# A macaron block on one core: another order at the start, halves in two banks at the end

## The reference

```
x = x + 0.5 * ffn(layernorm(x))
x = x + attention(layernorm(x))
x = x + 0.5 * ffn(layernorm(x))
ffn:       W1' = W1 + scale * m1(x), W2' = W2 + scale * m2(x)
           m1, m2: outer products of pairs of the sequence's tokens 1 to 16
           gelu(x W1'^T + b1) W2'^T + b2            (512 hidden units)
attention: 16 heads of 64; q and k divided by their rms, times q_rms_w, k_rms_w
           gate = softplus(k . u / |u| / 8)
           scores = q k^T / 8 - distance * softplus(omega) * slope * gate, causal
           softmax(scores) v, then Wproj
```

## Time and profile before

| | us |
|---|---|
| three runs | 773.44, 774.59, 774.47; median 774.47 |
| the profiled execution | 774.06 |
| its span, first to last instruction | 772.3 |
| TensorE busy | 737.8 (96%) |
| VectorE, ScalarE, GpSimd busy | 660.0, 645.6, 643.0 |
| mean granted clock of TensorE | 0.993 |

### The profile page before, as it was taken

One profiled execution on the slowest core, in us unless ns is written; L12 is line 12 of the kernel. 1 busy time (PEld: TensorE's weight loads), 2 busy tenths in 40 slices (PEclk: granted clock), 3 DMA queues, 4 the chain that ended last, 5 costly groups with the idle time before them and its releaser, 6 DMA issues.

```text
span 772.3 us, 25092 instructions
## 1 busy us (share of the span) xinstructions
PE 737.8 (96%) x9301; PEld 527.0 (68%) x9301; DVE 660.0 (85%) x2101; ACT 645.6 (84%) x1424; POOL 643.0 (83%) x751
## 2 busy tenths in 40 slices
PE   3969999999999999999999999999999999999988
PEld 1435777677667777577667777577766876677764
DVE  7699968987989779888989879897889889899955
ACT  5887889888998889987998889988898879986662
POOL 4265889889998989989999899989899899997780
PEclk9999999999999999999999999999999999999998
DMA  7113711533243423454053432434143432434430
GB/s 186 25 34 79 146 23 44 112 85 85 43 111 71 90 53 70 85 111 99 3 124 71 86 84 46 109 78 107 29 94 91 97 84 35 111 70 97 84 44 28
DMA packets 99602, 60.33 MB, mean 78 GB/s; under 512 B 74606, under 2 KB 86384, under 8 KB 99480
## 3 DMA queue, kind: packets, MB, share of 16 engines
q1 hardware_dynamic: 99320, 58.19, 35.1%
q10 hardware_dynamic: 160, 0.52, 0.2%
HBM read 4.74 MB, written 2.10 MB: 9 GB/s over the span
## 4 chain that ended last, share of the span: by engine, by line
PE 71%; ACT 12%; DVE 6%; POOL 5%; issue 4%; DMA 1%; SPq 0%; POOLq 0%; DVEq 0%; ACTq 0%
PE ps L1056 13%; PE ps L1058 12%; PE ps L1057 12%; PE ps L1176 8%; PE ps L1200 7%; PE ps L1201 7%; PE ps L1158 4%; ACT qk L991 3%; PE ps L1202 3%; ACT pt L1016 2%; POOL pt_l L825 1%; ACT hid L933 1%; DVE maxima L1516 1%; PE ps L1073 1%; ACT L933 1%
## 5 line engine op out<-in xcount | busy, mean ns | idle before, releaser
L825 POOL TENSOR_TENSOR pt_l<-pt 128x512 f16<-128x512 f32 x368 | 322.6, 906 | 35.5 <-ACT pt L1016 34.1
L1512 DVE CUSTOM_DVE_ANT_0 masked<-ps,causal_row 128x512 f16<-128x512 f32 x448 | 192.2, 486 | 26.3 <-PE ps L1176 25.4
L1016 ACT ACTIVATE pt<-ps 128x512 f32<-128x512 f32 (+1 forms) x384 | 174.4, 534 | 15.1 <-PE ps L1202 14.5
L851 POOL TENSOR_TENSOR qkn<-qkn,rs 128x512 f32<-128x512 f32 x128 | 130.8, 1049 | 29.6 <-ACT rs L955 29.0
L1200 PE MATMUL ps<-qk 128*128 128x512 f16 (+3 forms) x512 | 146.6, 299 | 0.0
L1201 PE MATMUL ps<-qk 128*128 128x512 f16 (+3 forms) x512 | 146.5, 299 | 0.0
L1056 PE MATMUL ps<-v_buf,pt 128*128 128x65 f16 x1280 | 129.8, 194 | 2.0 <-POOL pt_l L825 1.2
L1057 PE MATMUL ps<-v_buf,pt 128*128 128x65 f16 x1280 | 129.8, 193 | 0.0
L1058 PE MATMUL ps<-v_buf,pt_l 128*128 128x65 f16 x1280 | 129.6, 193 | 0.0
L1056 PEld LDWEIGHTS ps<-v_buf,pt 128*128 128x128 bf16 x1280 | 118.0, 98 | 7.4 <-issue 4.5
L1057 PEld LDWEIGHTS ps<-v_buf,pt 128*128 128x128 bf16 x1280 | 117.5, 98 | 1.7
(11 more groups left out here) (204 smaller groups left out, 1970.6 us busy)
## 6 DMA issues: line engine op xcount, KB each, us to landing
qk<-qk SPq DMA_DIRECT2D x128, 128.0 KB, 2.4
qk<-qk SPq DMA_DIRECT2D x62, 256.0 KB, 3.7
x_in<-in_L_attn_x SPq DMA_DIRECT2D x8, 256.0 KB, 3.1
out<-x_out SPq DMA_DIRECT2D x8, 256.0 KB, 2.5
qk<-qk SPq DMA_DIRECT2D x1, 1024.0 KB, 7.5
qk<-gtt SPq DMA_DIRECT2D x64, 8.0 KB
qk<-nmt SPq DMA_DIRECT2D x64, 2.0 KB
y_hl<-ytt SPq DMA_TRANSPOSE x63, 3.2
```

What stands on the lines that cost most here:

```text
L825: g.tensor_tensor(pt_l[:, h % 2, c], pt[:, h % 2, c], pt_h[:, h % 2, c], ALU.subtract).then_inc(s_pt_l, 1)
L851: g.tensor_tensor(qk, qk, r.unsqueeze(4).broadcast_to([P, 2, 2, 2, D]), ALU.mult).then_inc(s_qkn, 1)
L1016: a.activation(pt[:, h % 2, c], ps[:, j, 0:width], ACT.Exp).then_inc(s_exp, 1)
L1512: ins = d.tensor_tensor_reduce(masked[:, part.unit(s, i)[0], col:col + (ib + 1) * P], part.bank(s, i)[:, col:col + (ib + 1) * P], causal_r ...
```

## The change

It has these parts.

- **ScalarE's lead**: `gp` (the gelu table) goes from the front to behind `m`, directly before the first gelu; `setup` and `zt` go ahead of the qkv weights, `wo` behind `ln1` of the attention.
- **VectorE's lead**: `us` goes ahead of `ln2`, `uu` ahead of `setup`, `wq` 0 and 1 to either side of the first residual sum; the four square sums of the first quad (`qk` 0) all stand ahead of the gate weights.
- **Bias rows**: from VectorE to GpSimd, behind `m`, as four operations with a semaphore between them.
- **Gate weights by halves**: `gu2` 0 and 1, each with its product, reduction, cast and subtraction; `gu2` 1 stands behind the logits of the first half. `s_prepared` counts to 2, and the waits on it follow.
- **TensorE's lead**: `setup` before `m`; the six fillers go from the front to just ahead of the first hidden layer; the eighteen that stood behind the first ffn's output go among the projections (8 behind `qk` 1 1, 10 behind `v` 0 1); the spread of u (`uu`) goes directly behind that output.
- **The first sequence**: the same stages on each engine in a somewhat different order (`first`); for example `pv` 6 and `pv` 10 on TensorE now stand behind `s` 8 and `s` 12, which they preceded. `body` is the same.
- **Token halves in two banks**: the output of the first ffn and of the last, and the last output product of the attention, write token blocks 0 and 1 into their ring bank and 2 and 3 into a second one. `sum_halves` adds each half by itself and takes the next norm's statistics of three of the four blocks in between. The last store is two DMAs.
- **The last y parts in free operand memory**: the transposed y of pairs 6 and 7 goes to `y_end`, in `qk2`, so the last transfer and the last split don't wait for the product before.
- **The last head's low parts** (`pl` 15) are all three VectorE's; `yt` 6 on GpSimd comes directly behind `pl` 14.
- **TensorE's end**: `wp` 2 stands behind the last weighted sum and `yx`; eight fillers stand between `m` and `h` of the last ffn, and the thirteen at the very end are gone. On VectorE the sum of the sequence before (`add`, `c`, LAST) goes from ahead of `weff` into `m`, between the low part of z and the second half of `weff`.

```diff
 "tensor" lead:
-            ("warm", 0, 6, NEXT), ("zt", "a", NEXT), ("m", "a", NEXT), ("setup", NEXT), ("h", "a", NEXT),
-            ("out", "a", NEXT), ("warm", 1, 8, NEXT), ("warm", 1, 10, NEXT), ("zt", "att", NEXT), ("qk", 0, 0, NEXT),
+            ("zt", "a", NEXT), ("setup", NEXT), ("m", "a", NEXT), ("warm", 0, 6, NEXT), ("h", "a", NEXT),
+            ("out", "a", NEXT), ("uu", NEXT), ("zt", "att", NEXT), ("qk", 0, 0, NEXT), ("qk", 0, 1, NEXT),
...
 "tensor" final:
-            ("wp", 2, THIS), ("pv", 15, THIS), ("yx", THIS), ("wp", 3, THIS), ("out", "c", LAST), ("zt", "c", THIS),
-            ("m", "c", THIS), ("h", "c", THIS), ("out", "c", THIS), ("warm", 3, 7, THIS), ("warm", 2, 6, THIS),
+            ("pv", 15, THIS), ("yx", THIS), ("wp", 2, THIS), ("wp", 3, THIS), ("out", "c", LAST), ("zt", "c", THIS),
+            ("m", "c", THIS), ("warm", 2, 8, THIS), ("h", "c", THIS), ("out", "c", THIS),
...
 "scalar" lead:
-            ("gp", "a", NEXT), ("ln1", "a", NEXT), ("sel", NEXT), ("wq", 0, NEXT), ("zt", "a", NEXT), ("setup", NEXT),
+            ("ln1", "a", NEXT), ("sel", NEXT), ("setup", NEXT), ("zt", "a", NEXT), ("wq", 0, NEXT), ("m", "a", NEXT),
+            ("gp", "a", NEXT), ("h", "a", NEXT), ("wq", 1, NEXT), ("wq", 2, NEXT), ("ln1", "att", NEXT), ("wo", NEXT),
...
 "vector" lead:
-            ("ln1", "a", NEXT), ("ln2", "a", NEXT), ("us", NEXT), ("zl", NEXT), ("b2", NEXT), ("setup", NEXT),
+            ("ln1", "a", NEXT), ("us", NEXT), ("ln2", "a", NEXT), ("zl", NEXT), ("uu", NEXT), ("setup", NEXT),
...
+        SECOND_HALF = {"a": Y_BANK, "att": 0, "c": 1}
...
+        y_end = [qk2[:, 0, K1, :, :], qk2[:, 0, Q0, :, :]]
+        y_last = y_end[1]
...
+            def bias_rows(part, s, b):
+                pool.wait_ge(s_wffn, 16 * 7)
+                pool.wait_ge(s_w_l["a"], 1)
...
+                g.tensor_scalar(b2rows[top, :, :], b2ld[top, :].unsqueeze(1).broadcast_to([1, TB, C]), W_UP, None, ALU.mult).then_inc(s_b2_top, 1)
+                g.tensor_scalar(b2cut[low, :], b2ld[low, :], W_UP, None, ALU.mult).then_inc(s_b2_cut, 1)
...
+                g.tensor_scalar(b2ld[low, :], b2ld[low, :], W_UP, None, ALU.mult).then_inc(s_b2_up, 1)
...
+                g.tensor_tensor(b2rows[low, :, :], b2ld[low, :].unsqueeze(1).broadcast_to([1, TB, C]),
+                                b2cut[low, :].unsqueeze(1).broadcast_to([1, TB, C]), ALU.subtract).then_inc(s_b2, 1)
...
+                dve.wait_ge(s_wqk[hf], 64)
+                half_of, heads = slice(hf * 512, (hf + 1) * 512), slice(hf * HH, (hf + 1) * HH)
+                link(d.tensor_tensor(pairs(uk[:, half_of]), wqk_ld[:, 2 * hf:2 * hf + 2, 1, :].rearrange("p q (i n) -> p q i n", i=2),
+                                     pairs(ps[:, hf, :]), ALU.mult))
+                link(d.tensor_reduce(wu[:, heads], of_heads(uk[:, half_of]), AX.X, ALU.add))
+                link(d.tensor_copy(wu_h[:, heads], wu[:, heads]))
+                d.tensor_tensor(wu_l[:, heads], wu[:, heads], wu_h[:, heads], ALU.subtract).then_inc(s_prepared, 1)
...
+            def sum_halves(part, s, n, by, src, dst, next_stats):
+                for t in (0, TB // 2):
+                    if t == 0:
+                        part.full(dve, s)
+                    else:
+                        dve.wait_ge(s_second_half[n], 1)
+                    bank = part.bank(s) if t == 0 else ps[:, SECOND_HALF[n], :]
+                    blocks, cols = slice(t, t + TB // 2), slice(t * C, (t + TB // 2) * C)
+                    ins = d.scalar_tensor_tensor(dst[:, blocks, :].rearrange("p t c -> p (t c)"), bank[:, cols], by,
+                                                 src[:, blocks, :].rearrange("p t c -> p (t c)"), ALU.mult, ALU.add)
...
+                    if next_stats:
+                        for u in range(t, min(t + TB // 2, TB - 1)):
+                            d.bn_stats(stats[next_stats][:, u, :], dst[:, u, :])
...
+                        sp.dma_start(rows[:, 0:TB // 2, :], x_out[:, 0:TB // 2, :]).then_inc(s_out, 16)
+                        sp.wait_ge(s_second_half[n], 2)
+                        sp.dma_start(rows[:, TB // 2:TB, :], x_out[:, TB // 2:TB, :]).then_inc(s_out, 16)
```

More of the change, by code:

```diff
@@ L1101, in ffn_out @@
                 if b == 0 and n == "a":
+                    pe.wait_ge(s_b2_top, 1)
                     pe.wait_ge(s_b2, 1)
                 part.room(pe, s)
-                pe.matmul(part.bank(s), ones[:, :], b2rows[:, :, :].rearrange("p t c -> p (t c)"), start=True, stop=False)
+                for first, dst in ((0, part.bank(s)), (T // 2, ps[:, SECOND_HALF[n], :])) if shared(n, b) else ((0, part.bank(s)),):
+                    width = T // 2 if shared(n, b) else T
+                    pe.matmul(dst[:, first:first + width], ones[:, :], b2rows[:, :, :].rearrange("p t c -> p (t c)")[:, first:first + width],
+                              start=True, stop=False)
                 for r in range(FB):
@@ L1112, in ffn_out @@
                         c = slice(t * P, (t + 1) * P)
-                        mm = product(part.bank(s)[:, c], hid_h[:, r, c], hid_l[:, r, c], w2_h[:, w], w_l[:, 1, w], False,
-                                     r == FB - 1 and t == TB - 1)
-                part.filled_by(mm, s)
+                        second = shared(n, b) and t >= TB // 2
+                        dst = ps[:, SECOND_HALF[n], :] if second else part.bank(s)
+                        mm = product(dst[:, c], hid_h[:, r, c], hid_l[:, r, c], w2_h[:, w], w_l[:, 1, w], False,
+                                     r == FB - 1 and t == (TB // 2 - 1 if shared(n, b) and not second else TB - 1))
+                        if shared(n, b) and r == FB - 1 and t == TB // 2 - 1:
+                            part.filled_by(mm, s)
+                if shared(n, b):
+                    mm.then_inc(s_second_half[n], 1)
+                else:
+                    part.filled_by(mm, s)
             def project_qk(part, s, b, qd, t):
@@ L1188, in scores @@
                 n = b * H + h
+                if n == 0:
+                    pe.wait_ge(s_prepared, 2)
                 if h % QH == 0:
@@ L1459, in add_ffn @@
                     dve.wait_ge(s_out, 16 * b)
+                if shared(n, b):
+                    sum_halves(part, out, n, 0.5 / W_UP, src, dst, "att" if n == "a" else None)
+                    return
                 part.full(dve, out)
```

289 lines of the change are left out of this document (155 added, 134 removed).

## The result

The changed kernel takes 765.4 us (median of 4 runs, 763.98 to 766.36) against 773.96 (4 runs, 772.93 to 774.59) on the same chip: ratio 0.9893, 95% interval 0.9879 to 0.9907. The forecast was 764.2, its range 760 to 769. The profiled execution took 766.36 us with a span of 764.6, that is 7.7 us less than 772.3; it is the longest of the four.

What follows compares the result with a forecast made beforehand. The six middle sequences were taken as bound by TensorE, so gains lay in the two ends: lead 6.0 + first order 0 + tail 4.2 = 10.2 us off 774.06, 763.9; forecast 764.2 us, range 760 to 769.

Steps and rivals of the forecast that it cites:

- Table loads: Lead, ScalarE: two loads before z_a go, 2 x 1.28 = 2.6 us, of which 1.85 counts; z_a at 6.6.
- The first of them stands until 11.6: Lead: VectorE's first small operation beside GpSimd's clears waits 3.4 us, 8.2 to 11.6; hidden layer then at 16.4.
- rival 1: Lead: VectorE gets in between clears and scalings, hidden layer at about 14.0, total 760.5 us; chance 0.15.
- Hidden; without that cover they cost their 2.7: Lead: bias rows on GpSimd take 2.7 us, 16.4 to 19.1, covered because the output needs them at about 20.5.
- Scalings: Lead, GpSimd: with all four square sums first, the first two scalings come at 34.9 and 36.9 us.
- rival 2: Clock stays low in one or both hidden layers, costing 1.2 us in lead, 3.2 in tail: 768.6; chance 0.17.
- Cast stall: Lead: the first gate-weight half's cast on VectorE stalls 2.7 us beside running scalings, to 38.9; bounds 0 and 4.95.
- Transpose and transfers 5.3 us as before: Lead: from gates at 45.8 to first row maxima, 5.3 us; maxima at 51.4 against 57.91.
- rival 3: Lead: gate-weight halves cost more than they save, both casts standing behind full scaling runs: 767.8; chance 0.15.
- First order: First sequence: the new order is worth 0, bounds -0.5 to +1.5, TensorE being nearly full there.
- Rivals 4 and 5: First sequence's order stalls TensorE, 783 with seven heads, chance 0.04; later pipeline gives back the lead's gain, 769.3, chance 0.06.
- The moved sum: Tail, VectorE: the previous sequence's sum moves from ahead of weff, starting the hidden layer 0.6 us sooner.

Runs made afterwards that it cites:

- Experiment 5: Changed kernel with the gelu table's load back at the front of ScalarE's list: 768.07 us, ratio 0.9927.
- after: The changed kernel with the whole change, against the kernel before it: 765.4 us median, ratio 0.9893; profiled execution 766.36 us.
- the earlier trace: Profiled execution of the kernel before the change: 774.06 us, span 772.3.
- experiment 4: Changed kernel with FFN outputs and last attention product each in one bank again, one sum each, one store: 766.38 us, ratio 0.9897.
- experiment 1: Changed kernel with the bias rows back on VectorE, between the second weights and the hidden low parts: 764.8 us, ratio 0.9886.
- Experiment 2: Changed kernel with the bias rows first on GpSimd, before the weights' low part, and the four clears last: 762.26 us, ratio 0.9857.
- experiment 11: Changed kernel with the last head's first and third low parts back on GpSimd, pair 4's product ahead of the last weighted sum: 765.47 us, ratio 0.9893.
- experiment 6: Changed kernel with both halves of the gate weights in one block ahead of the third square sum: 767.44 us, ratio 0.9924.
- experiment 7: Changed kernel with the first sequence's order of before the change on all engines: 764.73 us, ratio 0.9889.
- experiment 10: Changed kernel with the sum of the sequence before back ahead of weff in the tail: 764.63 us, ratio 0.9891.
- experiment 3: Changed kernel without the eight fillers between adapted weights and hidden layer of the last ffn: 766.92 us, ratio 0.9915.
- experiments 6, 9 and 11: Number 9: changed kernel with four groups of fillers added, GpSimd's order untouched: 765.48 us, ratio 0.9896. Experiment 6 and experiment 11 have their own lines.

## Why the prediction was right, and which steps of it failed

The time was right within 1.2 us, the sum of the parts by 2.5 (10.2 against 7.7 in the profiled execution, which was 1.0 above its median). Part of that was luck: two errors of over 2 us in the lead, the wait for the clears and the low parts, had opposite signs and nearly cancelled.

**Table loads.** z_a 6.6 predicted, 6.67 measured; right. The sum counted the two ahead of z_a; a third, ahead of om_n, went too. Experiment 5 shows what they are worth at the end: 2.0 us in the trace, 2.6 in the medians. **Clears** 8.0 to 11.6 predicted, 8.09 to 11.74 measured.

**"The first of them stands until 11.6": failed by 1.6 us, and the hidden layer by 2.2.** om_e stood for 0.95 us, to 9.96, about one clear of 0.91; the mechanism is rival 1's, and the hidden layer began at 14.19, rival 1's 14.0, not 16.4. The Trainium skill, SBUF - State Buffer, "Who interferes with whom", read as I read it, has a wait of at most one clear. After, with 0.95 us, agrees; the earlier trace rows with 4.23 us and experiment 4 with 2.73 don't. One row was not enough to choose between the two ends. So the hidden layer's 5.8 us are 1.8 of table loads and 4.0 of VectorE's new order and the bias rows' leaving it; these 4.0 are read off the traces, since no run puts the rows and the square sums of u back at their former place.

**"Hidden; without that cover they cost their 2.7": failed.** The bias rows were 3.84 us (1.49, 0.69, 0.52, 1.14), inside the bounds of 1 and 4.3; I asked only who waits for their result. Only the last of them lies beside the low parts; the others pushed the diagonal there (18.48 us; without the rows it starts at 14.09, experiment 1). These two operations held up VectorE's two-operand subtractions, 5.12 us instead of 2.49. These 2.6 us took back all of the 2.3 by which gelu's end (19.04 against 21.3 predicted) was ahead of the forecast, and the 1.46 us wait of TensorE put the clock at risk. Experiment 2, which moves these five operations away from there, gets about 3 us back in the median; no run without that order does.

**zt_h_att** 28.3 predicted, 29.09 measured. **Scalings** from 34.9 predicted, 37.18 measured: 12 projections at 0.43 us each until 35.1, where I had full clock. That is rival 2's place in the lead, one layer later than it looked for it. In the execution of experiment 11, same lead, the clock was 1.00 from 20 to 25 us and the maxima came at 52.27, 2.2 us earlier; so of the 3.1 us by which 54.47 missed 51.4, about 2.2 goes with the clock of that one execution.

**Cast stall** 2.7 predicted; cast and subtraction took 0.89 and 0.96, against 0.17 each where no scaling ran: 1.5 us. **Gates** 45.8 predicted, 46.28 measured.

**"Transpose and transfers 5.3 us as before": failed.** The gates were only 0.5 us late, the maxima 3.1: from the one to the other it was 8.2 us. Before it was 5.7 (and 45.8 + 5.3 is 51.1, not 51.4).

```profile
52.24 0.24 POOL L859 TENSOR_TENSOR softplus<-lgp,lgl 128x32 f32<-128x32 f32 x1
47.58 2.10 PE L1198 MATMUL ps<-ident,qkn 128*128 128x128 f32 x16 [0.44 <-DVE qk L1574]
```

The first row is before's gates; there TensorE's first score product waited 0.28 us for their transfer. In after it stands with no wait behind 16 transposes of q and k (3.58 us, from 48.80) and six products: with the gates earlier, TensorE's list came last, and the transfer of the gates no longer did. The second row is the same 16 transposes in experiment 11, at a clock of 1.00; in after it was 0.61 from 48 to 52.4 us. There gates to maxima took 7.2 us. So 1.0 of the 2.9 us goes with the clock, and 1.9 is the step itself.

**The halves of the gate weights:** rival 3 said they cost. With after's order the casts stood 0.89 and 0.45 us and not through full runs of scalings; experiment 6 shows that the place of the halves gains about 2 us, and says nothing of the cut.

**First order** 0 predicted, 0 measured (experiment 7). Rivals 4 and 5 did not happen: the offset at the maxima (3.4) was never given back.

**Tail, 4.2 predicted, 3.7 measured.** Low parts and pair 4's product: 0.4 predicted, -0.1 measured (experiment 11). Halves at the attention sum: 0.7 predicted, 0.5 measured (experiment 4). The moved sum: 0.6 predicted, 0 measured (experiment 10); the step failed because I took it off the hidden layer's start, where the last thing to arrive at the output is VectorE's list, on which it still stands. Fillers and clock, and the halves at the output: z_a to the end is 3.3 us shorter, of which the fillers are 2.5 (experiment 3) and the halves 0.5. In the median the fillers are worth less, 0.0022 x 774 = 1.7 us, and the intervals overlap a little.

## What to carry to other kernels

When work moves to an idle engine, ask not only who waits for its result but what its operands' memory accesses do to the engines that work beside it: here 3.4 us of small GpSimd operations beside the low parts cost 2.6 us of VectorE, while four clears at the same place cost nothing. Of what was undone, the table load moved the time clear of the intervals, the place of the gate halves and the tail's fillers at their edge; the first order, the moved sum and the low parts' new engine did not. Not undone by themselves were VectorE's order in the lead, TensorE's fillers moved there, and the free operand memory. And when one link of a chain gets shorter, ask what arrives last behind it: the gates' transfer did before, TensorE's own list after. And where the granted clock differs between executions of the same instructions, one profile is not a measurement of it: take the median for what an edit is worth and the trace for how.

## What the runs showed of the hardware that I had not expected

- VectorE's f32-to-f16 subtraction of 128x512 runs at 0.62 us each beside GpSimd's clears (2.50 for four, experiment 2) and at up to 2.38 us beside its operations that read (5.12 for four, after). The tensor-scalar on 16 columns, though, did wait for clears.
- Beside four clears in a row that tensor-scalar lasted as long as one (0.95 us, after and eight other profiled executions) or three (2.73, experiment 4), with the same start; the bias copy of before until the end of the fourth (4.23). What decides between them stays open.
- With the same instructions up to 25 us, the granted clock from 20 to 25 us was 0.66 (after and experiment 10), 0.54 (experiments 3 and 7) and 1.00 (experiments 6, 9 and 11), behind the same 1.46 us of idle TensorE at 19.9 to 21.3.
- The column of the granted clock can miss a slow stretch: in the earlier trace rows it is 1.00 from 20 to 25 us while the products of the earlier trace rows start 0.43 us apart, as they do in the tail where it reads 0.50. Products 0.22 us apart are the surer sign of full clock.
- With gelu's table loaded in between, the logarithm and the exponential each fetch a table of their own (5.32 and 6.93, experiment 5); when the opening load's stands, there is no load before either (after). Each load is 1.28 us, the next instruction 0.01 to 0.02 us behind it.
